# Attention's weighing of values in three runs a group instead of five

## The reference, cut to what matters

```
scores = einsum('bhqd,bhkd->bhqk', q, k) / sqrt(32)     # causal
attn   = softmax(scores)
out    = einsum('bhqk,bhkd->bqhd', attn, v)
```

## Time and profile before

| | us |
|---|---|
| median of 3 runs | 3024.13 (3019.51 to 3024.2) |
| the profiled execution, as timed | 2997.19 |
| its span in the profile | 2995.4 |
| PE busy | 2899.0 (97%) |
| DVE busy | 2120.9 (71%) |
| POOL busy | 1837.7 (61%) |
| ACT busy | 1340.9 (45%) |

### The profile page before, as it was taken

One profiled execution on the slowest core, in us unless ns is written; L12 is line 12 of the kernel. 1 busy time (PEld: TensorE's weight loads), 2 busy tenths in 40 slices (PEclk: granted clock), 3 DMA queues, 4 the chain that ended last, 5 costly groups with the idle time before them and its releaser, 6 DMA issues. The chain is left out here.

```text
span 2995.4 us, 49806 instructions
## 1 busy us (share of the span) xinstructions
PE 2899.0 (97%) x16480; PEld 2159.9 (72%) x16480; DVE 2120.9 (71%) x5344; ACT 1340.9 (45%) x2436; POOL 1837.7 (61%) x1077
## 2 busy tenths in 40 slices
PE   8999999999999999999999989999999999989996
PEld 5788888766666666666666578887877888767875
DVE  6555555677777777777777588887878788846764
ACT  2222222156666666666666533223322333236764
POOL 1333222278888888888888157577656776755664
PEclk9999999999999999999999999999999999989998
DMA  7555555755665565555665332333223323148996
GB/s 255 201 193 199 190 182 182 228 122 131 134 136 115 115 134 133 134 116 116 135 136 136 112 127 75 109 100 103 82 80 104 118 84 95 60 142 211 232 237 119
DMA packets 281948, 420.53 MB, mean 140 GB/s; under 512 B 48463, under 2 KB 132687, under 8 KB 281742
## 3 DMA queue, kind: packets, MB, share of 16 engines
q1 hardware_dynamic: 259214, 384.22, 45.2%
q0 software_dynamic: 22528, 33.72, 5.8%
HBM read 263.38 MB, written 153.01 MB: 139 GB/s over the span
## 5 line engine op out<-in xcount | busy, mean ns | idle before, releaser
L1166 ACT ACTIVATE att_pt<-att_ps_p 128x512 f32<-128x512 f32 (+1 forms) x1024 | 524.5, 587 | 192.6 <-PE att_ps_p L1389 168.1
L247 DVE CUSTOM_DVE_ANT_0 att_ps_s<-att_ps_s,att_causal 128x512 f32<-128x512 f32 (+1 forms) x992 | 469.9, 504 | 188.5 <-PE att_ps_s L1304 188.3
L1386 PE MATMUL att_ps_p<-att_qs,att_ks 98*128 98x512 f32 (+3 forms) x1536 | 501.5, 366 | 8.6 <-ACT att_pt L1166 7.8
L1304 PE MATMUL att_ps_s<-att_ks,att_qs 96*128 96x512 f32 x1488 | 505.9, 368 | 2.2 <-DVE att_lower L253 0.6
L1105 POOL TENSOR_TENSOR att_gathered<-att_gathered,att_pt 128x2048 f32<-128x2048 f32 (+1 forms) x92 | 388.3, 4221 | 41.2 <-ACT att_pt L1166 36.4
L253 DVE TENSOR_REDUCE att_lower<-att_ps_s 128x1 f32<-128x512 f32 x496 | 340.0, 685 | 53.0 <-PE att_ps_s L1304 53.0
L1098 POOL TENSOR_TENSOR att_pt<-att_pt 128x1024 f32<-128x1024 f32 (+2 forms) x153 | 331.3, 2165 | 58.6 <-PE att_ps_o L1330 36.8
L1386 PEld LDWEIGHTS att_ps_p<-att_qs,att_ks 98*128 98x128 f32 x1536 | 270.0, 190 | 129.3 <-issue 80.7
L1912 POOL DMA_INDIRECT slot_info<-ffn_info,ffn_slot x256 | 277.2, 1083 | 113.1 <-issue 78.9
L1304 PEld LDWEIGHTS att_ps_s<-att_ks,att_qs 96*128 96x128 f32 x1488 | 273.6, 190 | 69.0 <-DVE att_rowmax L247 22.4
L577 POOL TENSOR_TENSOR qkv_x<-qkv_x,qkv_mod 128x512 f32<-128x512 f32 x60 | 83.5, 1392 | 368.4 <-DVE qkv_x L671 368.4
(11 more groups left out here) (311 smaller groups left out, 6552.2 us busy)
## 6 DMA issues: line engine op xcount, KB each, us to landing
att_qs<-qk_parts SPq DMA_DIRECT2D x96, 512.0 KB, 6.9
att_ks<-qk_parts SPq DMA_DIRECT2D x96, 512.0 KB, 12.8
qk_parts<-qkv_out_hi SPq DMA_DIRECT2D x128, 256.0 KB, 2.2
qk_parts<-qkv_out_lo SPq DMA_DIRECT2D x128, 256.0 KB, 2.4
qkv_x<-x SPq DMA_DIRECT2D x16, 1024.0 KB, 5.5
v_rows<-qkv_out_v SPq DMA_DIRECT2D x64, 256.0 KB, 2.3
att_vs<-v_rows SPq DMA_DIRECT2D x32, 512.0 KB, 16.2
o_parts<-att_o SPq DMA_DIRECT2D x64, 256.0 KB, 7.9
```

The costliest lines, as they stand in the source:

```text
L247: dve.tensor_tensor_reduce(part, part, self.causal[:, UNIT - (c1 - c0):UNIT], scale=1.0, scalar=MASKED, op0=ALU.add, op1=ALU.max, accum_ou ...
L1166: act.activation(tile(c)[:, h, col:UNIT], ps_p[(NPROB * prev.g + n) % NP][:, col:UNIT], ACT.Exp, scale=float(HD) ** -0.5).then_inc(exp_don ...
L1304: pe.matmul(bank("s", cur.g, i)[:, 0:c1 - c0], qs[cur.slot][0:STACK, h, t * P:(t + 1) * P], ks[cur.slot][0:STACK, h, c0:c1], start=True, s ...
L1386: last = pe.matmul(part[:, i * (UNIT - col):(i + 1) * (UNIT - col)], ks[prev.slot][:, h + i, kt * P:(kt + 1) * P], qs[prev.slot][:, h + i, ...
```

## The change

One line: chunks 0 to 3 are weighed together behind chunk 4, where only 2 and 3 were, and chunks 4 to 7 behind chunk 8, where only 6 and 7 were. The run behind chunk 0 stays. The places behind chunks 2 and 6 go.

```diff
-        WEIGHED_AT = {0: (8, 9, 10, 11), 2: (0, 1), 4: (2, 3), 6: (4, 5), 8: (6, 7)}
+        WEIGHED_AT = {0: (8, 9, 10, 11), 4: (0, 1, 2, 3), 8: (4, 5, 6, 7)}
```

## The result

| | us |
|---|---|
| predicted | 3007.7 (2998 to 3017) |
| after, median of 20 runs | 3018.0 (3000.04 to 3029.23) |
| before, median of 20 runs | 3024.32 (3017.13 to 3049.91) |
| ratio | 0.9962, 95% interval 0.9944 to 0.9980 |

The ratio is worth 11.5 us of 3024 (6 to 17): faster, as forecast, with 16.4 us forecast. In each trace the middle half of the 30 periods lies within 0.06 us, and a few periods are up to 0.7 us longer.

The account below looks back on a forecast made before the run. PE was taken to set the time. Gains of 0.39 us (late) and 0.13 us (early) a group, over 31 groups plus 0.28 in the last, make 16.4 us off 3024.13: 3007.7 us, range 2998 to 3017.

Parts of the forecast that it names:

- PE sets the time; no matmul is removed; what goes is the change of shape: In attention: PE busy 33.67 of 33.90 us a group; two changes to the 128*32 shape and back go.
- Price of a run, 0.39 us: Behind chunk 6: 0.15 us going in, 0.13 the way out, 0.11 behind it, together 0.39 us beside the columns.
- A longer run costs its columns and nothing else: Runs behind chunks 4 and 8: they grow only by their added columns, 1.51 and 1.72 us.
- Late half: Chunks 5 to 8: chunk 7 starts 2.11 us sooner, DVE and ACT follow; gain 0.39 us a group.
- Early half: Chunks 1 to 4: DVE can come only 1.50 to 1.64 us sooner, against 1.51 added; gain 0.13 us a group.
- POOL: Its adds start 3.87 us later within the group but cost nothing; the cover is 5 us a group.
- DVE as no limit: Rival, both halves: DVE doesn't hold PE back, gain 21 to 24 us, time 3000 to 3003; chance 13%.
- New stalls: Rival, long stretch of scores: PE stops at banks once or twice more a group, 3014 to 3020 us; chance 20%.
- Nothing: Rival: DVE's idle is needed elsewhere or shape change is charged by column; within 6 us of 3024; chance 10%.
- POOL as a slower way: Rival: POOL's chain of adds becomes the bound, each further us a group costing 31 us, e.g. 3039; chance 7%.
- The sum: All groups: 0.39 + 0.13 = 0.52 us a group, 16.1 us for 31 groups, 16.4 with the last group.

Follow-up runs that it names:

- early half alone: Against the kernel before: chunks 0 to 3 weighed together behind chunk 4, chunks 4 to 7 in two runs as before; period 33.76 us, ratio 0.9999.
- seven runs: Kernel before with two more weighing runs a group (single chunks behind 2, 3, 6, 7; pairs behind 4, 8): period 44.37 us, ratio 1.1017.

## Why the prediction was right, and where its numbers were off

- **PE sets the time; no matmul is removed; what goes is the change of shape.** Right. Busy PE falls from 33.66 to 33.22 us a group with the same instructions, at a clock of 1.00.
- **Price of a run, 0.39 us.** This is the term that was mis-sized: it measured 0.28 to 0.29 us. The way in and the product behind were compared with steps that follow a wide matmul, while at this place narrow ones meet. 31 × 0.10 = 3.1 us of the 3.7 us between 16.4 and 12.7.
- **A longer run costs its columns and nothing else.** The working drew this from two runs only, through which any line goes. It is right: with L261 out of the way the run behind chunk 8 takes 4.26 us, which is 2.54 + 1.72; that behind chunk 4 takes 4.01, or 2.50 + 1.51.
- **Late half: the others follow.** ACT and DVE did in the stretch. In the run DVE didn't, because of L261, the last maximum. The working did not look at it; by its account DVE had only to empty its banks. It cost PE 0.08 us at the transpose and gave most of that back in the tail; without the wait the period is 0.03 us shorter (33.45 for 33.48).
- **Early half: DVE allows 1.50 to 1.64 us.** Right by the traces, with the upper value: 0.14 us for 0.13, and after the change DVE doesn't idle between its first piece of chunk 1 and the run behind chunk 4. The timed ratio of the early half alone, 0.9999 (0.9977 to 1.0021), can't tell so small a gain from none.
- **POOL.** Its idle before the first add is 4.28 us for the 4.3 forecast, and only 0.18 us is left before the add of chunk 5. PE doesn't wait for its results. But the account asked only who waits for what POOL produces. While it adds, it also keeps out DVE's instruction with two inputs in SBUF, and for that the moment of each add matters, not only the time by which it is wanted.
- **Rivals.** DVE as no limit: out, by the early half alone (0.13, not 0.28). New stalls: out, but for 0.08 us. Nothing: out, by the period and by the interval of the ratio, which ends at 0.9980. POOL as a slower way: the right engine and the wrong mechanism. Its price was set at 1 us a group for each us of wait; in the seven runs 3.1 us of PE's wait cost 10.5 us a group, since the clock fell with it.
- **The sum.** 0.52 − 0.10 for the price, − 0.03 for L261, + 0.01 for the early half is 0.40, and 0.41 was measured. The time fell inside the range by its ratio; the interval of the ratio, 6 to 17 us, is too wide to tell 16.4 from 12.7.

## What to carry to other kernels

When a change moves one engine's work in time, list also which of its neighbour's instructions will now meet it, not only which results come late. Here the pair was a GpSimd add and a VectorE instruction with two inputs in SBUF. A wait that a long run covers is a debt: here 2.4 us were hidden behind a run of 4.3 us. With seven runs a wait of 3.97 us met a run of 2.5 us, and PE stood idle and then ran at half the clock. Price a removed change of shape against the same neighbours that will stand there afterwards, and take it away first where PE, not the engine behind it, has the pace.

## What the runs showed that was not expected

- A VectorE maximum of 16 columns with two inputs in SBUF took 0.17, 0.39, 1.09, 1.31, 2.39, 2.63 and 3.97 us, by where it met GpSimd's add of two SBUF tiles (3.5 or 4.5 us whole, 1.8 halved). Where it was longer than 0.17 it ended 0.03 to 0.04 us behind that add. As a reduction with one input 0.18 to 0.19 us in every group of five kernels.
- Around the end of a wait of 3.1 us without a matmul TensorE's granted clock fell to 0.50, and it stayed there for 17 us (14 the first time), in each group anew, though TensorE was busy for all but 3.3 of the 44.4 us.
- Going to the 128*32 shape and back cost TensorE 0.28 us where narrow matmuls stood around it.
